# Feed-forward stage of a two-layer decoder: GpSimd takes over the clamps of the rounded rows and of one weight block

## What is computed

```python
def _quant_weight(w):
    scale = jnp.mean(jnp.abs(w)) + EPS
    wq = jnp.clip(jnp.round(w / scale), -1.0, 1.0) * scale
    return w + jax.lax.stop_gradient(wq - w)

def _quant_act(x):
    scale = jnp.maximum(jnp.max(jnp.abs(x), axis=-1, keepdims=True), EPS) / 127.0
    xq = jnp.clip(jnp.round(x / scale), -128.0, 127.0) * scale
    return x + jax.lax.stop_gradient(xq - x)

def bitlinear(x, w):
    return jnp.einsum('bsi,oi->bso', _quant_act(x), _quant_weight(w))

gate = jax.nn.sigmoid(bitlinear(x, w_gate))     # w_gate, w_up: 1024 x 256
up = bitlinear(x, w_up)
h = gate * up
return bitlinear(h, w_down)                      # w_down: 256 x 1024
...
x = _layernorm(x + _L0_ffn_ref(x, L0_ffn_w_gate, L0_ffn_w_up, L0_ffn_w_down), axis=-1)
x = _layernorm(x + _L1_attn_ref(x, ...), axis=-1)
```

## Time and profile before

| | us |
|---|---|
| median of 3 runs | 751.31 |
| lowest, highest | 749.43, 752.69 |
| the profiled execution | 752.89 |
| span of its profile | 751.0 |
| busy: TensorE, DVE, ScalarE, GpSimd | 657.1, 485.7, 436.1, 199.8 |

### The profile page before, as it was taken

The page is one execution under the profiler, slowest core; times in us unless marked ns, Lnnn a source line. Parts: engine busy times, 40 slices in busy tenths (PEclk is TensorE's granted clock), DMA queues, the critical chain, the costliest instruction groups (busy, mean ns, idle before and its releaser), DMA issues.

```text
span 751.0 us, 13910 instructions
## 1 busy us (share of the span) xinstructions
PE 657.1 (87%) x4826; PEld 541.1 (72%) x4833; DVE 485.7 (65%) x1091; ACT 436.1 (58%) x1124; POOL 199.8 (27%) x364
## 2 busy tenths in 40 slices
PE   8798797998998998987987799999987799999950
PEld 6566577998998998863566688878875377878840
DVE  1567676469478477449876667576556567777735
ACT  2997857338448348457976647564433265656522
POOL 2455430021000000001233334344227312222225
PEclk9999999999999999999999999999999999999985
DMA  8996000220220232320020000000096201111114
GB/s 303 380 324 186 1 1 1 88 89 1 89 89 0 89 103 98 106 63 1 1 85 1 1 2 2 1 2 1 1 390 263 71 29 50 49 49 49 50 56 140
DMA packets 32226, 62.03 MB, mean 83 GB/s; under 512 B 2500, under 2 KB 26824, under 8 KB 29928
## 3 DMA queue, kind: packets, MB, share of 16 engines
q1 hardware_dynamic: 30152, 56.04, 22.2%
q0 software_dynamic: 2016, 5.22, 2.0%
HBM read 45.80 MB, written 15.55 MB: 82 GB/s over the span
## 4 chain that ended last, share of the span: by engine, by line
PE 59%; ACT 17%; DVE 14%; issue 3%; POOL 3%; DMA 3%; SPq 0%; POOLq 0%; ACTq 0%; DVEq 0%
PE banks L1758 37%; PE bank L1758 22%; ACT arena L766 5%; DVE U_split L1234 3%; ACT U_split L785 2%; ACT arena L1024 2%; DVE mx L1188 1%; POOL rstd L574 1%; POOL xs L670 1%; DMA ys<-arena 1%; ACT arena L804 1%; DVE fh L1411 1%; DVE arena L1408 1%; DVE bmx L1253 1%; ACT arena L978 1%
## 5 line engine op out<-in xcount | busy, mean ns | idle before, releaser
L1758 PE MATMUL banks<-U_split 128*128 128x512 f32 (+1 forms) x616 | 146.7, 350 | 5.0 <-DVE U_split L1234 2.7
L1758 PE MATMUL bank<-U_split 128*128 128x256 f32 (+1 forms) x864 | 115.6, 290 | 13.8 <-DVE U_split L1234 13.7
L1758 PEld LDWEIGHTS bank<-U_split 128*128 128x128 f32 x864 | 108.6, 194 | 17.8 <-issue 15.6
L1758 PEld LDWEIGHTS banks<-U_split 128*128 128x128 f32 x616 | 96.4, 190 | 22.2 <-issue 6.7
L785 ACT ACTIVATE U_split<-arena 128x1024 fp32r (+6 forms) x122 | 97.2, 821 | 12.6 <-DVE arena L1676 4.9
L1758 PE MATMUL banks<-cst,arena 128*128 128x128 f32 (+1 forms) x594 | 89.3, 277 | 14.5 <-POOL arena L647 9.6
L571 POOL TENSOR_SCALAR rstd<-mv 128x1 f32<-128x1 f32 x48 | 11.1, 230 | 295.5 <-DVE mv L1166 263.5
L1758 PEld LDWEIGHTS banks<-cst,arena 128*128 128x128 f32 (+1 forms) x594 | 68.7, 141 | 27.8 <-POOL arena L647 13.4
L1758 PE MATMUL banks<-arena 128*128 (+4 forms) x632 | 84.8, 382 | 3.3 <-DVE arena L1182 2.3
L1024 ACT ACTIVATE arena<-banks,dmx 128x128 f32<-128x128 f32 (+1 forms) x128 | 52.9, 424 | 45.8 <-DVE dmx L1521 45.7
L1758 PEld LDWEIGHTS banks<-arena 64*128 64x128 f32 (+3 forms) x632 | 61.3, 177 | 20.8 <-issue 9.0
(11 more groups left out here) (236 smaller groups left out, 1194.7 us busy)
## 6 DMA issues: line engine op xcount, KB each, us to landing
arena<-in_w_exp SPq DMA_DIRECT2D x8, 1536.0 KB
xs<-arena SPq DMA_DIRECT2D x8, 1032.0 KB
arena<-in_ctxT SPq DMA_DIRECT2D x4, 1601.0 KB, 6.7
arena<-in_ctx SPq DMA_DIRECT2D x4, 1536.0 KB
arena<-in_w_f SPq DMA_DIRECT2D x3, 1024.0 KB, 11.7
arena<-xs SPq DMA_DIRECT2D x23, 129.0 KB, 2.0
w_x<-in_w_x SPq DMA_DIRECT2D x9, 256.0 KB, 7.0
arena<-in_w_oh SPq DMA_DIRECT2D x1, 2048.0 KB, 8.8
```

The costliest lines, as they stand in the source:

```text
L1758: return nc.tensor.matmul(o, w, x, start=start, stop=stop, **k)
```

## The change

- GpSimd's list gets the clamp of the down weights (two instructions on 128x2048), behind the `rstd_of` of norm 14 and ahead of that of norm 15, and the clamps of all eight hidden tiles. From there on step t of its list is the clamp of tile t and then `rstd_of` for tile t-2.
- DVE's list loses both. Its rows, scales and factors of tiles 6 and 7 move from step 1 to step 2, their clamps from step 2 to step 3; ScalarE's two roundings of the same rows move from step 2 to step 3.
- ScalarE's rounding of tile t also waits for the clamp of tile t-1 (one buffer `hr`), DVE's `f_hidden(t)` for the rounding of tile t-2 (`hh`). The wait for `d_rot` goes, GpSimd's clamp for `f_hqT` (two buffers `hq`) is new.

```diff
--- before.py
+++ after.py
@@ -632,10 +632,25 @@
                 rstd_of(NT + 2 * b)
                 if b == 0:
                     d_turned()
+
+            pool.wait_ge(G["w_round"], 3)
+            g.tensor_scalar(w_f32[:, 2, :], w_f32[:, 2, :], MAGIC, 1.0, ALU.subtract, ALU.min).then_inc(G["pool_step"], 1)
+            steps[0] += 1
+            pool.wait_ge(G["pool_step"], steps[0])
+            g.tensor_scalar(w_ff[:, 2, :], w_f32[:, 2, :], -1.0, None, ALU.max).then_inc(G["w_tern"], 1)
             rstd_of(2 * NT - 1)
 
-            for n in range(NT):
-                rstd_of(2 * NT + n, centre=True)
+            def f_hidden_quant(t):
+                pool.wait_ge(G["f_hround"], t + 1)
+                if t >= 2:
+                    pool.wait_ge(G["f_hqT"], t - 1)
+                g.tensor_scalar(hq[:, t % 2, :], hr, MAGIC, QMAX, ALU.subtract, ALU.min).then_inc(G["f_hq"], 1)
+
+            for t in range(NT + 2):
+                if t < NT:
+                    f_hidden_quant(t)
+                if t >= 2:
+                    rstd_of(2 * NT + t - 2, centre=True)
 
             pool.wait_ge(G["ld_x01"], 160)
             g.tensor_scalar(bg[:, :], bg[:, :], 0.5, None, ALU.mult).then_inc(G["const_set"], 1)
@@ -975,9 +990,11 @@
                     f_gate(t + 1)
                 if t < NT:
                     act.wait_ge(G["f_hsc"], t + 1)
+                    if t > 0:
+                        act.wait_ge(G["f_hq"], t)
                     a.activation(hr, hh[:, t % 2, :], ACT.Identity, scale=fh[:, t % 3, 3:4],
                                  bias=magic[:, :]).then_inc(G["f_hround"], 1)
-                if t == 2:
+                if t == 3:
                     f_round(NT - 2)
                     f_round(NT - 1)
                 if 0 < t < NT:
@@ -1323,8 +1340,6 @@
             def w_quant(n):
 
                 dve.wait_ge(G["w_round"], n + 1)
-                if n == 2:
-                    dve.wait_ge(G["d_rot"], 3 * KV1)
                 link(v.tensor_scalar(w_f32[:, n, :], w_f32[:, n, :], MAGIC, 1.0, ALU.subtract, ALU.min))
                 v.tensor_scalar(w_ff[:, n, :], w_f32[:, n, :], -1.0, None, ALU.max).then_inc(G["w_tern"], 1)
 
@@ -1402,6 +1417,8 @@
 
             def f_hidden(t):
                 j, i = t % 2, t
+                if t >= 2:
+                    dve.wait_ge(G["f_hround"], t - 1)
                 for c in range(2):
                     dve.wait_ge(G["f_sig"], 2 * t + c + 1)
                     dve.wait_ge(G["f_gu"], 4 * t + 2 * c + 2)
@@ -1415,11 +1432,6 @@
                 v.tensor_tensor(fh[:, i % 3, 3:4], fh[:, i % 3, 2:3], fs[:, i, 4:5], ALU.mult).then_inc(G["f_hsc"], 1)
                 v.tensor_tensor(fh[:, i % 3, 4:5], fh[:, i % 3, 1:2], wsc[:, 2:3], ALU.mult).then_inc(G["dve_step"], 1)
                 steps[0] += 1
-
-            def f_hidden_quant(t):
-                j = t % 2
-                dve.wait_ge(G["f_hround"], t + 1)
-                v.tensor_scalar(hq[:, j, :], hr, MAGIC, QMAX, ALU.subtract, ALU.min).then_inc(G["f_hq"], 1)
 
             def f_out(t):
                 n = 2 * NT + t
@@ -1458,8 +1470,7 @@
                     d_query(0)
                 if t == 0:
                     b_ln(2 * B - 1)
-                if t == 1:
-                    w_quant(B - 2)
+                if t == 2:
 
                     for n in (NT - 2, NT - 1):
                         ln_end(NT + n)
@@ -1468,8 +1479,7 @@
                     f_factors(NT - TPB, NT)
                 if t > 1:
                     f_out(t - 2)
-                f_hidden_quant(t)
-                if t == 2:
+                if t == 3:
                     f_quant(NT - 2)
                     f_quant(NT - 1)
```

## The result

The changed kernel took a median of **783.32 us** (4 runs, 776.54 to 784.03) against 751.22 for the kernel before on the same chip: a ratio of 1.0438, interval [1.0397, 1.0478]. It is 32 us slower. The profiled execution took 782.9 us for a span of 780.9, so 29.9 us of span are to be found.

The account below looks back on a forecast made before the run. It took ScalarE's queue, a ring of waits through GpSimd, as the bound. Rounding(2) 0.5 us earlier, then turns of 6.5 us plus 0.5 for small clamps shift the stage's end by +2.6: 753.9 us, range 750.3 to 757.6.

Parts of the forecast that it names:

- part 2: Eight hidden clamps moved from DVE to GpSimd: 1.11 us each, a line through two sizes; ends 0.69 and 1.90.
- part 1: Two weight clamps moved to GpSimd: 1.97 us each, costing nothing; at 3.8 us each, holding tile 0's clamp 2.6 us.
- The upper end of 1.90 us: GpSimd's hidden clamp: highest price considered, taken from its 128x1024 product of two tensors.
- The ring: Feed-forward stage: rounding, GpSimd's clamp, rstd, ScalarE's rows, then next rounding; 6.5 us a tile against 5.6 and 6.2.
- the signs named: Feed-forward stage: clamps 1.11 us, weight clamps before 339 us, rows' wait 5 to 8, turns 6.5, last copy at 389.7.
- the case that the prediction set apart: Feed-forward stage: the round of waits is there with another clamp in it, so the price alone is wrong.
- Rival A: GpSimd's clamp is dearer, each 0.1 us more costing 0.5 us; at 1.90 us, 759.9 us; chance 0.27.
- the forecast's own 2.6: End of TensorE's last turn-back in the feed-forward stage: 389.75 us instead of 387.14, a shift of +2.6 us.
- Part 5: Factors, roundings and small clamps of tiles 6 and 7 a step later: 0 to 0.5 us, 0.5 taken.
- Part 4: New waits of ScalarE's rounding for the previous clamp and DVE's product for an older rounding: cost nothing.
- Rivals B and C: DVE's relief counts: B, clamp near 0.7 us, 751.3 us, 0.17 shared; C, large gain, 743.3 or 747.6 us, 0.06.
- Rival D: Behind the stage: the shift is taken up at a transfer waited for anyway, 751.3 us; chance 0.17, shared.

Follow-up runs that it names:

- experiment 7: The changed kernel with all GpSimd clamps as two multiplies and the factors, roundings and small clamps of tiles 6 and 7 back in place: 754.35 us.
- experiments 2 and 3: The changed kernel with all GpSimd clamps as two multiplies (2), 756.11 us; with only the hidden clamps as multiply and add (3), 765.0 us.
- experiment 6: The kernel before with the weight clamp still on DVE but made earlier, ahead of the last cross attention output: 748.80 us.
- experiment 4: The kernel before with parts alone: hidden clamps with the moved order, 776.07 us; weight clamps, 752.14 us; factors a tile later, 752.71 us.
- experiment 8: The changed kernel with hidden clamps as multiply and add, rstd ahead of the clamp, factors in their old place, weight clamp early on DVE: 751.65 us.

## Why the prediction was wrong

The step that failed is one term, the price of the clamp (part 2, and part 1 with it). The rows that the line was drawn through are two multiplies (L647 of the kernel before, `ALU.mult, ALU.mult`), and the instruction to be priced is subtract with minimum. "Same operation, same engine" was false: it was the same opcode in the profile, with other operations inside. For a clamp in the form of those rows the line was right to 0.06 us (1.11 estimated, 1.05 measured), and for the weights too (1.97 and 1.91). For the form in the diff it was 2.5 us short in each of eight clamps, and 8.6 us short in the two of the weights (12.5 instead of 3.9). The upper end of 1.90 us was no bound either: it was the row of another opcode, with two tensors as inputs.

**The ring** was right. Its terms beside the clamp come to 5.4 us; with 3.64 they give 9.0, measured 9.13 to 9.25. With a clamp of 1.05 they give 6.4, measured 6.55 to 6.66 in experiment 7; in experiments 2 and 3, with the factors still late, the turns from tile 2 to tile 6 spread from 6.53 to 7.38. Of the signs named, that of the ring came: L952's idle time grown (14.4 us, forecast 5 to 8 for the cheap clamp), released by L579. Those that hang on the price did not: turns of 6.5 us, the weight clamps done before 339 us, the last turn-back copy at 389.7 us (it came at 417.6). This is the case that the prediction set apart, the ring there with another clamp in it.

**Rival A** had the mechanism and the direction, at 0.27, and each 0.1 us for 0.5 us: 2.5 us more give 12.6, and with the forecast's own 2.6 that is 15.2, where the six turns from tile 1 on grew by 16.3. Its time, 759.9, was capped by the same false bound, and so was the range.

**The weight clamps** (part 1) were to end by 338.1 or at worst by 341.8; they ended at 344.1, in an execution in which the stage began 2.7 us earlier. Their cost was not 2.6 us at the dear end but some 7 of the 33, because tile 0's clamp stood behind them and TensorE behind that.

**TensorE's clock** was no term of the sum at all. After the idle of 9.64 us the eight matmuls took 1.73 us more than at full clock, and the way out 3.2 us more, so some 5 of the 33 us were the clock's; of these the first 1.7 may in part be no effect of the change, as experiment 6 shows. The same is seen in miniature in experiment 4 (+0.94). The stage's clock was 0.81.

**Part 5** was called nothing, or 0.5; alone it cost 3 us, 0.4% [0.23 to 0.58%]. The due time checked was that of the factors. What was moved past was not checked: tile 0's output stood behind them in DVE's list.

**Part 4**, the new waits, cost nothing visible: the rounding's own idle time in the changed kernel is 1.1 us in all, ended by DVE's scale.

**Rivals B and C** rested on DVE's relief being worth something. The runs show no such gain: 2.4 us of work less in step 1 gave nothing (experiment 6), and with all hidden clamps at the lowest price reached, 1.05 us, the stage is 56.3 us long against 55.7 and the time 0.3% more (experiment 8). A clamp of 0.7 us, on which B was built, no run has. **Rival D** did not come: what follows the stage is as long as before.

By the ratios, each known to about 2 us, the loss reads as a ladder: +33 us as changed; hidden clamps in the fast form +16; weight clamps too +6; factors back +4; rstd first and weights back on DVE, early, +2. The last two steps are within their error. How much of each rung is the clock and how much the order was not separated.

## What the runs showed of the hardware

**Some DVE instructions are longer beside one of GpSimd, by anything from a part of what GpSimd has still to do to all of it.** DVE in the changed kernel, while GpSimd's L637 ran from 331.55 to 338.67 and L640 from 338.75 to 344.12, and then while L647 ran from 373.60 to 377.23:

```profile
335.13 0.97 DVE L1432 TENSOR_TENSOR fh<-fh,fs 128x1 f32<-128x1 f32 x1
...
340.29 2.12 DVE L1432 TENSOR_TENSOR fh<-fh,fs 128x1 f32<-128x1 f32 x1
...
374.04 0.74 DVE L1303 TENSOR_SCALAR arena<-arena 128x256 bf16<-128x256 f32 x1 [6.75 <-ACT arena L836]
375.51 0.29 DVE L1303 TENSOR_SCALAR arena<-arena 128x256 bf16<-128x256 f32 x1 [0.73 <-ACT arena L836]
```

L1432 takes 0.16 us undisturbed, and here 0.97 and 2.12; L1303 takes 0.29, and here 0.74. So these are longer, and the instructions around them are not. But L1432 was through at 336.10 and 342.41, with 2.6 and 1.7 us of GpSimd's instruction to come, and the second L1303 ran its 0.29 us inside the clamp. In the kernel with the weight clamps alone, on the other hand, DVE's clamp met the same first pass, which ended at 338.07 there:

```profile
336.81 1.81 DVE L1428 TENSOR_SCALAR arena<-arena 128x1024 bf16<-128x1024 f32 x1 [0.23 <-ACT arena L984]
```

It took 1.12 us more than its 0.69, nearly the 1.26 that GpSimd still had. The Trainium skill, "SBUF — State Buffer", section "Who interferes with whom", has the ports that DVE and GpSimd share held for the whole instruction by whichever issues first when DVE is in a two-port mode, and has a DVE instruction with two SBUF inputs (L1432) contend with one of GpSimd that reads SBUF. The last row agrees with a hold to the end; the four before it don't. What decides, and in which mode L1303 ran, no run here shows. GpSimd's own instruction can be the longer one as well: with the hidden clamps alone, its first clamp took 4.34 us instead of 3.64. The forecast's 0.5 us for the meeting of small clamps (part 5) is near the 0.45 of L1303.

**On GpSimd the pair of operations sets the price**, at 128x512: multiply with multiply or with add 0.62 us, a cast 0.61; one operation alone (multiply, subtract or maximum) 1.49 or 1.50; subtract or multiply with minimum 1.92 or 1.93. The Trainium skill, "GPSIMD Engine Reference", section "Engine selection", has operations with one input at roughly line rate. DVE clamps 1024 columns in 0.69 us; the fast forms come to 1.05 and agree within a factor of 1.5, the clamp at 3.64 does not, by 5.3.

## What to carry to other kernels

A duration is a price for its operations, not for its opcode: look in the code at which operations the priced row has, and if none has those of the diff, say that the price is open upward, or measure it with a probe in an idle gap before choosing a bound. On GpSimd, write a pass of this kind as multiply with multiply or multiply with add where the arithmetic allows. A busy share says where room is, not what a relief is worth: here the full engine was relieved of every hidden clamp, and at the lowest price reached the kernel was still 0.3% slower; the clamp had stayed in the round of waits and only changed its queue. When a step is moved later, check both its own due time and that of everything it now stands ahead of. And where an edit lets TensorE stand idle, count the clock too: its matmuls can be slower behind the pause.
